# Decoder layer, head of the TensorE program: transposes of batch 0 ahead of the context's first projection, second projection behind the values, five warm-up products instead of two

## The reference

```python
x = x + linear_attention(layernorm(x), q_w, q_b, k_w, k_b, v_w, v_b, o_w, o_b)   # 16 heads, elu + 1 as the feature map
x = x + softmax(mask((ctx @ Wq.T + bq) @ (ctx @ Wk.T + bk).T / 8 * layernorm(x))) # ctx is 4 x 256 x 64
x = x + ffn(layernorm(x))   # Hadamard, up and gate (256 -> 1024), silu, Hadamard, down (1024 -> 256)
```

## Time and profile before

| | us |
|---|---|
| median of 3 runs | 125.3 (125.2 to 125.59) |
| the profiled execution, its own time | 125.14 |
| its span, first to last instruction in the trace | 123.3 |
| PE busy | 119.2 (97%) |
| DVE busy | 82.7 (67%) |
| ACT busy | 71.6 (58%) |
| POOL busy | 68.5 (56%) |

### The profile page before, as it was taken

The page is one execution under the profiler, slowest core; times in us unless marked ns, Lnnn a source line. Parts: engine busy times, 40 slices in busy tenths (PEclk is TensorE's granted clock), DMA queues, the critical chain, the costliest instruction groups (busy, mean ns, idle before and its releaser), DMA issues.

```text
span 123.3 us, 2272 instructions
## 1 busy us (share of the span) xinstructions
PE 119.2 (97%) x804; PEld 107.0 (87%) x804; DVE 82.7 (67%) x207; ACT 71.6 (58%) x158; POOL 68.5 (56%) x89
## 2 busy tenths in 40 slices
PE   5999999999999999999999999999999999999990
PEld 2259999999999999999989999988888888889890
DVE  1399989899889899899998959674522332220521
ACT  1785696679748689888491479983135444280000
POOL 2228959979979966959802605762005574066000
DMA  3999910280000000000000110000110000000121
GB/s 123 316 377 423 398 76 5 53 330 3 8 0 0 0 5 3 0 0 0 0 5 0 43 45 0 5 0 0 39 46 3 5 0 0 0 0 0 54 73 43
DMA packets 3823, 7.64 MB, mean 62 GB/s; under 512 B 544, under 2 KB 1952, under 8 KB 3684
## 3 DMA queue, kind: packets, MB, share of 16 engines
q1 hardware_dynamic: 3806, 7.50, 16.8%
q10 hardware_dynamic: 6, 0.01, 0.0%
HBM read 6.46 MB, written 1.05 MB: 61 GB/s over the span
## 4 chain that ended last, share of the span: by engine, by line
PE 97%; POOL 0%; DVE 0%; issue 0%; POOLq 0%
PE bank L1283 19%; PE bank L1295 18%; PE bank L1300 11%; PE bank L1177 10%; PE bank L1304 5%; PE bank L1201 5%; PE bank L1239 5%; PE bank L1155 4%; PE bank L1115 4%; PE bank L1211 3%; PE bank L1221 3%; PE bank L1309 2%; PE bank L1146 2%; PE bank L1247 2%; PE bank L1128 1%; PE bank L1259 1%
## 5 line engine op out<-in xcount | busy, mean ns | idle before, releaser
L1283 PE MATMUL bank<-xh_home,wug 128*128 128x256 f32 x192 | 24.7, 285 | 0.0
L1283 PEld LDWEIGHTS bank<-xh_home,wug 128*128 128x128 f32 x192 | 23.6, 191 | 0.1
L1295 PE MATMUL bank<-xh_home,wug 128*128 128x512 f32 x96 | 22.0, 390 | 0.0
L1295 PEld LDWEIGHTS bank<-xh_home,wug 128*128 128x128 f32 x96 | 18.0, 188 | 3.7
L969 DVE SCALAR_TENSOR_TENSOR back<-bank,sc_up,back 128x512 f32<-128x512 f32 x8 | 6.0, 751 | 15.0 <-PE bank L1295 15.0
L351 POOL TENSOR_TENSOR hs<-back,hs 128x256 fp32r<-128x256 f32 x8 | 5.9, 740 | 17.0 <-ACT hs L614 16.9
L345 POOL TENSOR_TENSOR hs<-front,hs 128x256 fp32r<-128x256 f32 x16 | 11.5, 740 | 6.6 <-ACT hs L599 6.6
L1177 PE MATMUL bank<-watt,xT 128*128 128x256 f32 x96 | 14.0, 288 | 0.0
L1177 PEld LDWEIGHTS bank<-watt,xT 128*128 128x128 f32 x96 | 12.3, 189 | 0.9 <-ACT xT L492 0.7
L606 ACT ACTIVATE back<-bank,vecs 128x512 f32<-128x512 f32 x8 | 5.5, 688 | 12.1 <-PE bank L1295 12.1
L1300 PE MATMUL bank<-wdh,hs 128*128 128x512 f32 x48 | 12.5, 396 | 0.0
(11 more groups left out here) (132 smaller groups left out, 257.6 us busy)
## 6 DMA issues: line engine op xcount, KB each, us to landing
wd_a<-in_w_d SPq DMA_DIRECT2D x1, 1024.0 KB, 8.0
front<-in_w_ug SPq DMA_DIRECT2D x2, 512.0 KB, 8.5
back<-in_w_ug SPq DMA_DIRECT2D x2, 512.0 KB, 3.8
out<-x_res SPq DMA_DIRECT2D x8, 128.0 KB, 1.9
wd_b<-in_w_qkv SPq DMA_DIRECT2D x3, 256.0 KB, 4.5
x_res<-in_x SPq DMA_DIRECT2D x1, 512.0 KB, 6.0
x_res<-in_x_first SPq DMA_DIRECT2D x1, 385.0 KB, 3.1
back<-in_ctx_t SPq DMA_DIRECT2D x1, 260.0 KB
```

The costliest lines, as they stand in the source:

```text
L1283: ins = mm(dst[:, n * SEQ:(n + 1) * SEQ], wug[:, wa, k, at_col + j * P:at_col + (j + 1) * P], xh[b][:, xb, k, :], start=(i == 0), stop=(i ...
L1295: ins = mm(dst[:, :].rearrange("p (b s) -> p b s", s=SEQ), wug[:, wa, k, at_col + j * P:at_col + (j + 1) * P], xh_home[:, PAIR, cols], sta ...
```

## The change

The transposes of batch 0 move ahead of u(0); u(1) moves from in front of K(0) to behind V(0); three more warm-up products are issued behind mx. ACT and DVE follow: `u_copy` and one `negate_mean` move ahead of `exp_k(0)`, `u_hi(1)` behind `normalise(1, 1)`, and on DVE `u_lo(1)` behind `v_add(0)`. The lists of POOL and SP are the same.

```diff
-WARM, WARM_MORE = 8, 2
+WARM, WARM_MORE = 8, 5
...
-HEAD = (("mx", 0), ("u", 0), ("T1", 0), ("u", 1), ("K", 0), ("V", 0), ("Q", 0), ("T1", 1), ("SC", 0),
+HEAD = (("mx", 0), ("T1", 0), ("u", 0), ("K", 0), ("V", 0), ("u", 1), ("Q", 0), ("T1", 1), ("SC", 0),
...
             u_hi(0)
             w_hi('wq', 2)
-            u_hi(1)
-            exp_k(0)
             u_copy()
             negate_mean(1, 1)
+            exp_k(0)
+            normalise(1, 1, xn)
+            u_hi(1)
             negate_mean(1, 2)
-            normalise(1, 1, xn)
             xT_hi(1)
...
             u_lo(0)
-            u_lo(1)
             elu_k(0)
             v_add(0)
+            u_lo(1)
             ln_stats(1, 3)
```

## The result

| | before | changed |
|---|---|---|
| median of the runs, us | 125.3 (125.2 to 125.59, 4 runs) | 126.02 (125.98 to 126.05, 4 runs) |
| profiled execution, us | 125.14 | 126.05 |
| its span, us | 123.3 | 124.2 |
| PE busy, us | 119.2 | 120.1 |

The ratio is 1.0057, with a 95% interval of 1.0043 to 1.0071: the change makes the kernel 0.7 us slower, and the profiled execution 0.9 us. In a later session, 12 runs of the changed kernel had a median of 126.07, and of before 125.42 beside it, ratio 1.0041 (1.0002 to 1.008).

What follows compares the result with a forecast made beforehand. The prediction took PE, 97% busy, as the bound; warm-up 0, transposes 0, u(1) 0.86 and the rest 0 made 126.0 profiled, plus 0.16 for the median: 126.15, stated as 126.1, range 125.4 to 126.6.

Steps and rivals of the forecast that it cites:

- Its size of 0.86 us on the chain: u(1) behind V, where PE has no hole: its 0.86 us is added in full.
- the forecast of 126.1: Whole kernel: median of the runs at 126.1 us, likeliest case, 63%.
- the 0.26 us won in front of K: Ahead of K: K begins 0.26 us earlier, but its low products still wait for DVE until 9.12; worth 0.
- the clock rise at 6.2: Warm-up products behind mx: TensorE goes from 1.2 to 2.4 GHz at 6.2 us, as in the profile before.
- a sign of error: Five warm-up products behind mx: if they show the clock rising at another time than 6.2, the prediction is wrong.
- three more cost about 0.3 + 0.22 + 0.22: Behind mx: the three added warm-up products end at 6.8 or a little before, costing the transposes about 0.1 us.
- xn be ready at 6.70: Ahead of batch 0's transposes: DVE has xn ready at 6.70, so the transposes begin at 6.8.
- A late rise of the clock: Rival, head of the kernel: clock rises at 9.8, change costs about 0.55 us, 125.85 us; chance 10%.
- The gate didn't move: Rival, ahead of K's low products: DVE's low part of x starts earlier, up to 0.33 us gained, 125.8; chance 12%.
- DVE's wait for the rows' transfer: Rival, DVE ahead of v_add: idle time not covered by 0.4 us of slack, 126.5 to 126.7; chance 9%.
- five products would make the kernel faster than before: Rival, u(0) to K: three more warm-up products avoid a late clock rise, saving 1.5 us, 124.7; chance 6%.

Runs made afterwards that it cites:

- e2: Kernel before with only u(1) moved behind V(0), using the changed kernel's ACT and DVE lists; median 126.83 us, ratio 1.0106, profiled 126.14.
- e12: Kernel before with batch 0's transposes ahead of u(0) and five warm-up products behind mx instead of two, u(1) still ahead of K; median 125.33 us.
- r_after: The changed kernel run and profiled again, nothing altered, in a later session; median 126.07 us, profiled 126.03.
- e4: The changed kernel with two warm-up products behind mx instead of five; median 126.95 us, ratio 1.0114, profiled 126.02.
- e3: Kernel before with only batch 0's transposes moved ahead of u(0), two warm-up products kept; median 125.34 us, ratio 1.0012.
- e11: Kernel before with batch 0's transposes ahead of u(0) and three warm-up products behind mx instead of two; median 125.27 us, ratio 0.9993.
- e1: Kernel before with five warm-up products behind mx instead of two, nothing moved; median 125.67 us, ratio 1.0026.
- e9: Changed kernel with two warm-up products, and DVE's low part of batch 0's x ahead of the values' weights' low part; median 126.47 us, ratio 1.0052.
- e7: Kernel before with no warm-up products behind mx, the eight in front kept; median 127.85 us, ratio 1.0069.
- e6: Kernel before with only DVE's low part of batch 0's x ahead of the values' weights' low part; median 125.78 us, ratio 1.0029.

## Why the prediction was right

**The mechanism.** u(1) filled a wait ahead of K and stands in the open behind V: shown by e2, which has that move alone (profiled 126.14), and by e12 and r_after, which lack and have it (0.74 us). Its size of 0.86 us on the chain was right to the digit; at Q the profile shows 0.94, with 0.06 of it from an xn that came later. The medians are nearer each other (0.72 us): before, the runs lay 0.16 us above the profiled execution, and the prediction carried that over; in the changed kernel they lie 0.03 below it. So a part of the good agreement of 126.02 with the forecast of 126.1 is two small misses, 0.05 up and 0.19 down.

**The gate.** K's low products start at 9.12 before, and at 9.20, 9.18, 9.15 and 9.26 in the changed kernel, r_after, e4 and e2, with transposes that started between 6.46 and 7.26. That DVE's list alone holds them is shown in e4, whose chain runs through it while ACT is 0.27 us ahead. In the changed kernel ACT's high part ended at 8.42 and DVE's low part began at 8.45, so that the list and the late transposes hold it together; in e2 ACT's part is on the chain, and ended at 8.49. I said that the 0.26 us won in front of K would only lengthen the wait, to 0.5; in the changed kernel nothing was won, since the transposes started later than thought: K began at 8.47 instead of 8.36, and the wait was 0.19.

**The warm-up products.** They cost nothing that shows behind the gate, as predicted, but not as worked out. I let the clock rise at 6.2 and the products end at 6.8; they ran at 1.2 GHz until about 6.9 and ended at 7.36. The prediction named this as a sign of error, and the step "three more cost about 0.3 + 0.22 + 0.22" was wrong by 0.5 us. I also let xn be ready at 6.70, though PE's transposes can begin behind its first half (6.46 to 6.50 in e3, e4, e11 and e12). So the products held the transposes for 0.7 us and not for 0.1. That this was hidden is luck: the transposes' result came 0.03 us before DVE was free. e1, where both halves of u stand behind the five products as well, pays 0.38 in its profile.

**The rivals.** A late rise of the clock is real (10.2 in e9, which cost 0.84 us there, and the prediction's case took 9.8), and e7 shows a fall; I gave it 10% on the ground that three runs of before lay close together, which was thin: in the later sessions 20 of 89 runs of before lay far above the rest, for a cause that isn't shown. The gate didn't move in the changed kernel. DVE's wait for the rows' transfer was covered, with 0.36 us left against the 0.4 that I had counted (0.21 in r_after). That five products would make the kernel faster than before fell. They do make this order of steps faster and steadier than two products do, by 0.9 us in the median (e4), and the runs of e11 and e12 lie closer together than those of e3; the prediction had no term for that.

**What stays open.** e11 and e12 gave runs within 0.6 us of each other, and e3, which is e11 with one warm-up product less, runs from 125.17 to 128.61. Three profiles show two things that move the head of a kernel from run to run, the clock (e7, e9) and a late context (e6), but there is no profile of the highest runs, so what the spread comes from isn't settled. No version here beats the kernel before clearly; e11 ties with it.

## What to carry to other kernels

On the engine that is never idle, a step is free only where it stands in a wait, so before moving one out ask what will wait in its place. Moving the step that feeds a gate earlier gains nothing while another engine's list holds the gate; read that list back until it stops being back to back. Dummy products ahead of the first useful work are free until that work's input is ready, and beyond that only as far as a later gate hides them; their length depends on a clock whose rise differs between executions. Judge them by many runs and not by one profile: here they showed as nothing in the profiles and as 0.9 us in the median.

## What the runs showed of the hardware

- TensorE's first rise from 1.2 to 2.4 GHz, read from the pace of equal products, came near 4.0 us in e12, 4.6 in e4, 4.8 in e7, 6.0 in e1, 6.2 before, 6.9 in the changed kernel and in r_after, and 10.2 in e9, though all begin with the same eight products at 1.3 us. The granted clock in the profile says 1.00 in that stretch throughout.
- A later fall does show in it: 0.50 from about 8.2 to 11.6 us in e7, where PE had stood still for 1.09 us before 6.2. In e4 a hole of 0.85 us brought no fall.
- The Trainium skill, "TensorE: Matmul & The Clock Gate", part 1, says that how many products run at the low clock differs between runs of one kernel. The traces agree: in e12, e4 and e7 the clock rose at 4.0, 4.6 and 4.8 us, before anything that PE does in them differs from the kernels in which it rose at 6.0 or later.
- A matmul group that stops in the middle loses more than the idle time shown: six products took 1.08 us with a stop of 0.22 in the weight loads (before), and 0.71 without (e3).
- The context's transfer landed at 6.1 in e7 and 6.85 in e6, issued at the same moment (1.62, 1.63) into the same queue.
